# Layer 0's second activation: integer codes transposed by DMA in place of TensorE transposes

## The chip, the cores and the metric
One Trainium2 chip, one core. The metric is the device time of one execution in microseconds (us); three runs of the kernel before gave 379.6, 379.04 and 378.78, median 379.04. An execution under the profiler took 380.96 us.

## The reference
Input: x of 8 sequences x 512 tokens x 256 features. Two layers, each x = x + ffn(cond(x)). In layer 0, cond is an adapter chosen by a language id (256 to 64, ReLU, back to 256, residual) and a layer norm. The feed-forward part is two "bitlinear" maps with GELU between them:

```python
w_scale = clip(mean(abs(W)), EPS, None)
Wq = clip(round(W / w_scale), -1, 1) * w_scale           # ternary weights
x_scale = clip(max(abs(x), axis=-1), EPS, None)          # one per token
xq = clip(round(x * (127 / x_scale)), -128, 127) * (x_scale / 127)
y = einsum('bnd,hd->bnh', xq, Wq) + b                    # 256 -> 1024, GELU, 1024 -> 256
```

Layer 1 has a linear map chosen by a subject id, and a feed-forward part of the same kind with a depthwise convolution of three taps and SiLU in the middle.

## The kernel before, in words
Tokens lie on the 128 partitions. A block is 128 tokens; a pair is two blocks (k = 0 and 1); a batch (one sequence) is two pairs; there are 16 pairs. Every engine has its own program, written out by hand and executed in order; semaphores tie them. Layer 0 is a software pipeline of slots: slot (i, sp) works on pair 2i+sp in stage 0 (adapter, layer norm), on the pair before in stage 1 (rounding and transposing z), on the one before that in stage 2 (`up1`, `gelu`, `absmax1`, `scale1`, `inverse1`, `round1`) and on the one three back in stage 3 (`transpose1`, `untranspose`, `down1`, `final1`). I call (i,0) an even slot and (i,1) an odd one. At the end of an odd slot `adapter_in` (TensorE, L1133) computes the adapter's first map for the next batch; `adapter_out` (L1145) its second, once a slot; VectorE adds the result to the tokens (L809).

Stage 2 ends with `round1` on GpSimd (POOL): it multiplies GELU's output by the token's scale and adds the constant `ROUND`, 3*2^22 + 0x6600, in fp32, so that the low 16 bits of each word are the fp16 number 1536 + q, q the rounded integer. In stage 3 TensorE transposes those halves, 8 times 128x128 fp16 into one PSUM bank (`transpose1`, L1191); ScalarE (ACT) takes 1536 off again and writes q as bf16 to `q1T` (`untranspose`, L511); `down1` (L1200) multiplies by the ternary weights `w_dn0` in 8 matmuls that add up in PSUM; VectorE scales, adds the residual and writes `x1` (`final1`, L958), and SP stores x1 (L345).

SP issues all loads of layer 0. Its slots are: in an even slot `load_adapter_in(i+1)` (xT, cw1, cb1 of the next batch), in an odd one `load_tokens(i+1)` (cw2 at L323, cb2 at L324, the tokens xtok at L328, gamma and beta at L331 and L332); then in both the store of the pair in stage 3. Each of these buffers exists once, so a load waits until the present batch is through with it. A load that depends on a language id is preceded by a `value_load` of the id into a register. In layer 0, SP has no other work; i runs from 0 to 6 for the loads. Behind the last loads come `load2(0)` and the last stores.

POOL's order in a slot is `split_scales`, `residual` (L664), `scale_of_up`, `round1` of block 0, `inverse_deviation`, `round1` of block 1. VectorE's order is in `slot` at L898 to L928. Between the layers, `seam` writes out by hand how the last pairs of layer 0 mix with the first batch of layer 1.

Of the kernel before, what the change touches and what calls it, by code (L numbers as in the profile page):

```python
# [10 lines left out]
F16 = mybir.dt.float16  # L11
BF16 = mybir.dt.bfloat16
I32 = mybir.dt.int32

P = 128

# [1 line left out]
OFFSET = 1536.0  # L18
ROUND = float(3 << 22) + 0x6600
QMAX = 127.0  # L20
QEPS = 1e-5
LN_EPS = 1e-5


def build_program(nc, t):
# [12 lines left out]
    with ExitStack() as ctx:  # L38
        def sb(name, shape, dt=F32):
            return ctx.enter_context(nc.sbuf_tensor(name, shape, dt))  # L40

        def sem(name):
            return ctx.enter_context(nc.semaphore(name))
# [21 lines left out]
        idb = sb("idb", [P, P], BF16)  # L65
        ones = sb("ones", [P, P])
        nhalf = sb("nhalf", [P, 2])
        ids_sb = sb("ids_sb", [1, 2 * B], I32)
        raw_all = sb("raw_all", [P, 4, KD * H])
        raw = [raw_all[:, n, :] for n in range(4)]  # L70
# [49 lines left out]
        qs1 = [sb(f"qs1_{k}", [P, 1]) for k in range(2)]  # L120
        dq1 = [[sb(f"dq1_{r}_{k}", [P, 1]) for k in range(2)] for r in range(2)]
        r1 = [sb(f"r1_{k}", [P, H]) for k in range(2)]
        q1T = [sb(f"q1T{k}", [P, KH, P], BF16) for k in range(2)]
        xb = sb("xb", [P, PAIRS, 2, D])

# [4 lines left out]
        BANK_W = [7, 1, 7, 1]  # L130

        s_const = sem("s_const")
        s_ident = sem("s_ident")
        s_ones = sem("s_ones")
        s_hone = sem("s_hone")
# [37 lines left out]
        s_s1 = sems("s_s1", 2)  # L173
        s_qs1 = sems("s_qs1", 2)
        s_r1 = sems("s_r1", 2)
        s_t1 = sems("s_t1", 2)
        s_q1T = sems("s_q1T", 2)
        s_dn = sems("s_dn", 2)
        s_x1 = sems("s_x1", 2)
# [122 lines left out]
        def _(sp):  # L302
# [16 lines left out]
            def load_tokens(b, s):  # L319
# [11 lines left out]
                sp.dma_start(gam[:, :], t["gamma"][bass.ds(lang, 1), :].to_broadcast([P, D])).then_inc(s_ldgb, 16)  # L331
                sp.dma_start(bet[:, :], t["beta"][bass.ds(lang, 1), :].to_broadcast([P, D])).then_inc(s_ldgb, 16)  # L332

            def slot(i, sp_):

                if not isinstance(i, int) or 0 <= i < B - 1:
                    if sp_ == 0:
                        load_adapter_in(i + 1)
                    else:
                        load_tokens(i + 1, 2 * i + 2)  # L340
                if (c := in_slot(i, sp_, 3, PAIRS)):

                    n, par, h = c
                    sp.wait_ge(s_x1[1], n + 1)
                    sp.dma_start(item(scratch, h)[:, 2 * par:2 * par + 2, :], x1[par][:, :, :]) \  # L345
                        .then_inc(s_st1[par], 16)

            def load2(b):
# [56 lines left out]
        def _(act):  # L405
# [27 lines left out]
            def slot(i, sp):  # L433
                a1, a2, b_, c_ = (in_slot(i, sp, lag, PAIRS) for lag in range(4))

                def round_z():

                    n, par, h = a2
                    act.wait_ge(s_qsz, n + 1)
                    wait(act, s_zT, n)  # L440
                    for k in range(2):
                        ins = act.activation(rz[:, k, :], z[par][:, k, :], ACT.Copy, scale=qsz[par][:, k:k + 1],
                                             bias=ROUND)
                    ins.then_inc(s_rz, 1)
# [12 lines left out]


                second = isinstance(i, int) and (i, sp) == (1, 0)
                coming = a1 if second else in_slot(i, sp, -1, PAIRS) if sp == 1 else None  # L460
                if isinstance(i, int) and (i, sp) == (0, 1):
                    coming = None
                if second:
                    if b_:
                        gelu(b_, 0)
                    if coming:
                        adapter_hidden(coming)
                    if a2:
                        round_z()
                        untranspose_z()  # L470
                    if b_:
                        gelu(b_, 1)
                    return
                if b_:
                    gelu(b_, 0)
                if c_:
                    untranspose(c_, 0)
                if a2:
                    round_z()
                if b_:  # L480
                    gelu(b_, 1)
                if c_:
                    untranspose(c_, 1)
                if a2:
                    untranspose_z()
                if coming:
                    adapter_hidden(coming)
# [9 lines left out]
            def gelu(b_, k):  # L497
# [4 lines left out]
                wait(act, s_r1[k], n)  # L502
                act.activation(g1[k][:, :], bank(BANK_UP + 2 * k, 2), ACT.Gelu,  # L503
                               scale=dqz[par][:, k:k + 1]).then_inc(s_gelu[k], 1)

            def untranspose(c_, k):

                n, par, h = c_
                act.wait_ge(s_t1[k], n + 1)
                wait(act, s_dn[k], n)  # L510
                act.activation(q1T[k][:, :, :].rearrange("p k c -> p (k c)"),  # L511
                               bank16(BANK_T1, F16)[:, :], ACT.Copy, bias=-OFFSET).then_inc(s_q1T[k], 1)

            def lead(b, k):
                act.wait_ge(p_xT[k], b + 1)
# [40 lines left out]
            def seam():  # L556
                slot(B, 0)
                gelu(pair(PAIRS - 1), 0)
                lead(0, 0)
                untranspose(pair(PAIRS - 2), 0)  # L560
                gelu(pair(PAIRS - 1), 1)
                lead(0, 1)
                untranspose(pair(PAIRS - 2), 1)
                untranspose(pair(PAIRS - 1), 0)
                untranspose(pair(PAIRS - 1), 1)

            def slot2(s):
                on(lead_scales, s - 1)
# [33 lines left out]
        def _(pool):  # L602
# [7 lines left out]

            pool.memset(ones[:, :], 1.0).then_inc(s_ones, 1)
            pool.memset(nhalf[:, :], -0.5).then_inc(s_ident, 1)

            pool.memset(bias9b[:, :], 0.0).then_inc(s_b9z, 1)
            for k in range(2):
# [4 lines left out]
            def slot(i, sp):  # L620
# [56 lines left out]
                if b_:  # L677
                    round1(b_, 1)

            def round1(b_, k):  # L680

                n, par, h = b_
                wait(pool, s_t1[k], n)
                pwait(s_qs1[k], n + 1)
                pool.tensor_scalar(r1[k][:, :], g1[k][:, :], qs1[k][:, 0:1], ROUND, ALU.mult, ALU.add) \  # L685
                    .then_inc(s_r1[k], 1)

                pwait(s_x1[k], n - 1)
                pool.tensor_scalar(dq1[par][k][:, :], s1[k][:, :], ws[:, 1:2], 0.0, ALU.mult, ALU.add) \
                    .then_inc(s_dq1[k], 1)  # L690

            def round_y(b, k):
# [60 lines left out]
                on(tap_sum, s, 0)  # L753
                on(middle_tap, s, 2)

            run(slot, seam, slot2, pool)

        @block.vector
        def _(dve):
# [351 lines left out]
        def _(pe):  # L1111
# [66 lines left out]
                    ins = pe.matmul(o, c[:, k, :], bias9b[:, m * 512:(m + 1) * 512], start=False, stop=True)  # L1178
                ins.then_inc(s_up[k], 1)

            def transpose1(c_, k):
                n, par, h = c_
                if isinstance(n, int) and (n, k) == (0, 0):

                    pe.wait_ge(s_tern[1], 1)
                    pe.wait_ge(s_wsc, 7)
                pe.wait_ge(s_r1[k], n + 1)
                wait(pe, s_q1T[1 - k], n if k == 0 else n + 1)
                r16 = r1[k][:, :].bitcast(F16)
                for c in range(KH):  # L1190
                    ins = pe.transpose(bank16(BANK_T1, F16)[:, c * P:(c + 1) * P],  # L1191
                                       r16[:, 2 * c * P:2 * (c + 1) * P:2], id16[:, :])
                ins.then_inc(s_t1[k], 1)

            def down1(c_, k):
                n, par, h = c_
                pe.wait_ge(s_q1T[k], n + 1)
                wait(pe, s_x1[1 - k], n if k == 0 else n + 1)
                for c in range(KH):
                    ins = pe.matmul(bank(BANK_DN)[:, k * D:(k + 1) * D], q1T[k][:, c, :], w_dn0[:, c, :],  # L1200
                                    start=(c == 0), stop=(c == KH - 1))
                ins.then_inc(s_dn[k], 1)

            def slot(i, sp):
# [16 lines left out]
                    return  # L1221
                if b_:
                    up1(b_, 0)
                if c_:
                    transpose1(c_, 0)
                if a1:
                    adapter_out(a1)
                if b_:
                    up1(b_, 1)
                if c_:  # L1230
                    transpose1(c_, 1)
                if a2:
                    transpose_z(a2)
                if c_:
# [108 lines left out]
            def seam():  # L1343
                slot(B, 0)
                up1(pair(PAIRS - 1), 0)
                transpose_x(0, 0)
                transpose1(pair(PAIRS - 2), 0)
                up1(pair(PAIRS - 1), 1)
                linear(0, 0)
                transpose_x(0, 1)  # L1350
                transpose1(pair(PAIRS - 2), 1)
                down1(pair(PAIRS - 2), 0)
                linear(0, 1)
                down1(pair(PAIRS - 2), 1)
                transpose1(pair(PAIRS - 1), 0)
                spread_scales(0)
                transpose1(pair(PAIRS - 1), 1)
                transpose_y(0)
                down1(pair(PAIRS - 1), 0)
                down1(pair(PAIRS - 1), 1)  # L1360
# [87 lines left out]
```

## Time and profile before

| | |
|---|---|
| median of 3 runs | 379.04 us (378.78 to 379.6) |
| profiled execution | 380.96 us, its span 379.2 us |
| mean granted TensorE clock | 0.923 |
| layer 0, one batch (two slots) | 16.73 us |
| busy: TensorE / VectorE / ScalarE / GpSimd | 79% / 81% / 65% / 72% |

The span runs from the first instruction to the last. Times in the views below are microseconds from its start unless marked ns. PE is TensorE, PEld its weight loads, DVE VectorE, ACT ScalarE, POOL GpSimd, SPq the queue of SyncE that issues DMAs. Ends of pipelined matmuls are modelled, so busy times of PE overlap a little; the chain of waits gives the net time of a pass.

### The profile page before, as it was taken

How to read it: one execution, taken by the hardware profiler on the slowest of the kernel's cores; microseconds unless marked ns; L12 is line 12 of the kernel's file. 1: busy time of each engine (PE TensorE's matmuls, PEld its weight loads, DVE VectorE, ACT ScalarE, POOL GpSimd, SP SyncE). 2: the span in 40 equal slices, each digit the busy share in tenths (PEclk: the TensorE clock that was granted, in tenths of full speed). 3: DMA queues.
4: the chain of work that ended last, by engine and by line, in shares of the span. 5: the costliest groups of instructions: out<-in, count | busy, mean ns of one | idle time of the engine just before them, and what ended most of it. 6: DMA issues, size and time to landing. Idle time of an engine off the chain costs nothing.

```text
span 379.2 us, 7190 instructions
## 1 busy us (share of the span) xinstructions
PE 298.0 (79%) x2104; PEld 206.4 (54%) x2104; DVE 306.6 (81%) x649; ACT 246.1 (65%) x325; POOL 272.0 (72%) x433
## 2 busy tenths in 40 slices
PE   0449598999999898894482969898898979778694
PEld 0125356556565565472251647676776767556573
DVE  0875979899999999755169889999899999989563
ACT  3354657666676767553122678797979888788583
POOL 1342576777677777535055999999999999999921
PEclk9858989999999999996676889999999999989799
DMA  8980232424243330400542110014050502121201
GB/s 223 262 275 14 72 122 87 162 71 152 92 119 125 116 118 28 126 28 29 179 170 82 55 43 0 31 62 147 16 185 26 181 30 71 42 71 42 86 28 69
DMA packets 29421, 36.36 MB, mean 96 GB/s; under 512 B 6582, under 2 KB 22718, under 8 KB 29383
## 3 DMA queue, kind: packets, MB, share of 16 engines
q1 hardware_dynamic: 25142, 31.50, 25.6%
q10 hardware_dynamic: 4240, 4.41, 4.2%
q8 instruction: 17, 0.28, 0.3%
q14 instruction: 22, 0.17, 0.2%
HBM read 27.51 MB, written 8.39 MB: 95 GB/s over the span
## 4 chain that ended last, share of the span: by engine, by line
PE 35%; POOL 29%; issue 20%; DVE 6%; DMA 5%; ACT 3%; ACTq 1%; POOLq 0%; DVEq 0%; SPq 0%
POOL mid L712 12%; POOL raw_all L719 8%; PE banks L1200 8%; PE banks L1177 6%; POOL xb L696 5%; PE banks L1133 4%; PE banks L1178 3%; PE banks L1191 3%; PE banks L1145 3%; DMA raw_all<-in_w2b 3%; PE banks L1269 2%; DMA convb<-in_convb 2%; PE banks L1339 1%; DVE x L958 1%; PE banks L1157 1%
## 5 line engine op out<-in xcount | busy, mean ns | idle before, releaser
L719 POOL TENSOR_TENSOR raw_all<-raw_all,mid 128x1024 f32<-128x1024 f32 x32 | 77.0, 2407 | 3.7 <-DVE raw_all L1003 2.1
L685 POOL TENSOR_SCALAR r<-g,qs 128x1024 f32<-128x1024 f32 x32 | 36.0, 1124 | 41.9 <-DVE qs L949 41.7
L536 ACT ACTIVATE banks<-xb,taps 128x512 f32<-128x512 f32 x64 | 42.9, 687 | 30.6 <-DVE xb L996 30.5
L712 POOL TENSOR_SCALAR mid<-xb,taps,convb 128x512 f32<-128x512 f32 x64 | 49.3, 778 | 14.5 <-DVE xb L996 14.4
L503 ACT ACTIVATE g<-banks,dqz 128x1024 f32<-128x1024 f32 x32 | 35.5, 1109 | 31.2 <-PE banks L1178 29.8
L996 DVE TENSOR_TENSOR xb<-banks,dqb 128x512 f32<-128x512 f32 x64 | 42.5, 685 | 12.0 <-PE banks L1302 11.8
L1003 DVE SCALAR_TENSOR_TENSOR raw_all<-xb,taps,banks 128x512 f32<-128x512 f32 x64 | 46.9, 742 | 0.7 <-ACT banks L536 0.5
L934 DVE TENSOR_REDUCE am<-g 128x1 f32<-128x1024 f32 x32 | 38.7, 1208 | 5.9 <-ACT g L503 5.8
L1302 PE MATMUL banks<-yT,tern 128*128 128x512 bf16 x128 | 38.7, 410 | 2.8 <-DVE raw_all L1003 1.7
L1200 PE MATMUL banks<-tern,q1T 128*128 128x256 bf16 x256 | 35.3, 283 | 6.0 <-DVE x L958 6.0
L1009 DVE TENSOR_REDUCE am<-g 128x1 f32<-128x1024 f32 x32 | 38.6, 1206 | 1.6 <-ACT g L542 1.6
L1177 PE MATMUL banks<-tern,qT 128*128 128x512 bf16 x128 | 38.1, 379 | 0.9 <-ACT qcT L455 0.9
L542 ACT ACTIVATE g<-banks 128x1024 f32<-128x1024 f32 x32 | 32.6, 1018 | 8.6 <-POOL r L725 4.2
L1313 PE MATMUL banks<-id,raw_all 128*128 128x128 f32 x256 | 35.5, 284 | 0.6 <-ACT g L542 0.5
L1339 PE MATMUL banks<-tern,q1T 128*128 128x256 bf16 x256 | 35.0, 282 | 0.8 <-DVE o L1030 0.7
L511 ACT ACTIVATE q1T<-banks 128x1024 bf16<-128x1024 f16 x32 | 32.6, 1017 | 4.5 <-PE banks L1191 4.5
L1313 PEld LDWEIGHTS banks<-id,raw_all 128*128 128x128 f32 x256 | 31.0, 147 | 5.7 <-ACT g L542 1.5
L553 ACT ACTIVATE q1T<-banks 128x1024 bf16<-128x1024 f16 x32 | 32.6, 1020 | 1.5 <-PE banks L1325 1.5
L1200 PEld LDWEIGHTS banks<-tern,q1T 128*128 128x128 bf16 x256 | 23.5, 101 | 18.0 <-ACT q1T L511 7.4
L1269 PE MATMUL banks<-wl,x2T 128*128 128x256 f32 x128 | 32.7, 400 | 0.8 <-issue 0.7
L1325 PE MATMUL banks<-id,r 128*128 128x128 f16 x256 | 20.5, 225 | 11.6 <-POOL r L725 9.9
L1269 PEld LDWEIGHTS banks<-wl,x2T 128*128 128x128 f32 x128 | 24.7, 199 | 7.9 <-ACT x2T L517 2.4
(102 smaller groups left out, 630.8 us busy)
## 6 DMA issues: line engine op xcount, KB each, us to landing
xT<-in_xT SPq DMA_DIRECT2D x8, 512.0 KB, 3.7
xtok<-in_x SPq DMA_DIRECT2D x8, 512.0 KB, 3.6
x_after_layer<-x SPq DMA_DIRECT2D x16, 256.0 KB, 2.1
x<-x_after_layer SPq DMA_DIRECT2D x8, 512.0 KB, 4.3
xr<-x_after_layer SPq DMA_DIRECT2D x8, 512.0 KB, 3.7
out_y<-o SPq DMA_DIRECT2D x32, 128.0 KB, 1.7
wl<-in_cwl SPq DMA_DIRECT2D x8, 256.0 KB, 3.8
raw_all<-in_w1a ACTq DMA_DIRECT2D x1, 1024.0 KB, 5.1
```

The source lines that it names most:

```text
L536: act.activation(bank(BANK_U + f % 2), apad[:, f, 2:S + 2], ACT.Copy, scale=taps[:, f, 2:3]).then_inc(p_last, 1)
L712: pool.tensor_scalar(mid[f // 2 % 2][:, f % 2, :], apad[:, f, 1:S + 1], taps[:, f, 1:2], convb[:, f:f + 1], ALU.mult, ALU.add).then_inc(p_ ...
L719: pool.tensor_tensor(c[:, 2 * q:2 * q + 2, :], c[:, 2 * q:2 * q + 2, :], mid[q % 2][:, :, :], ALU.add).then_inc(p_sum, 1)
L934: dve.tensor_reduce(am1[k][:, :], g1[k][:, :], AX_X, ALU.max, apply_absolute_value=True) \
L996: dve.tensor_tensor(apad[:, f, 1:S + 1], bank(BANK_U + f % 2), dqb[b % 2][:, :], ALU.mult) \
L1003: dve.scalar_tensor_tensor(out=conv[b % 2][:, f, :], in0=apad[:, f, 0:S], scalar=taps[:, f, 0:1], in1=bank(BANK_U + f % 2), op0=ALU.mult, ...
L1177: pe.matmul(o, q[:, k, j, :], w_up0[:, j, m * 512:(m + 1) * 512], start=(j == 0), stop=False)
L1200: ins = pe.matmul(bank(BANK_DN)[:, k * D:(k + 1) * D], q1T[k][:, c, :], w_dn0[:, c, :], start=(c == 0), stop=(c == KH - 1))
L1269: ins = pe.matmul(bank(BANK_Y)[:, a * D:(a + 1) * D], x2T[:, 2 * k + a, j, :], wl1[par][:, j, :], start=(j == 0), stop=(j == KD - 1))
L1302: ins = pe.matmul(bank(BANK_U + f % 2), w_up1[:, k, f * P:(f + 1) * P], yT[b % 2][:, k, :], start=(k == 0), stop=(k == KD - 1))
L1313: ins = pe.transpose(bank(BANK_C + f // KT)[:, (f % KT) * P:(f % KT + 1) * P], conv[b % 2][:, f, k * P:(k + 1) * P], id32[:, :])
L1339: ins = pe.matmul(bank(BANK_D2)[:, (k % 2) * D:(k % 2 + 1) * D], q2T[k % 2][:, f, :], w_dn1[:, f, :], start=(f == 0), stop=(f == KH - 1))
```

## The change
For the second activation of layer 0 only (pair by pair, both blocks):

- `round1` on POOL writes q + 128 as a 16-bit unsigned integer (`r1u`, the first half of the old buffer). It now waits for the block's previous DMA transpose in place of the TensorE transpose.
- SP gets `transpose1`: for each block one DMA transpose of 128 x 1024 16-bit elements from `r1u[k]` to `q1T[k]`. TensorE's `transpose1` and ScalarE's `untranspose` are gone, also from the seam.
- SP's slot is reordered: in an even slot `load_adapter_in`, the transposes of blocks 0 and 1, the store; in an odd slot the transpose of block 0, `load_tokens`, the transpose of block 1, the store.
- `down1` reads the transposed integers as fp16 bits: the integer n is then n * 2^-24. A ninth matmul with the constant -128 * 2^-24 (`uncode`) and the column sums of the ternary weights (`colsum0`) takes the 128 off. The factor 2^24 goes into `dq1`.
- POOL computes `colsum0` once, with three additions after slot (1,0).

```diff
+        colsum0 = sb("colsum0", [P, 4, D], BF16)
+        r1u = [r1[k][:, 0:H // 2].bitcast(U16) for k in range(2)]
...
+            def transpose1(b_, k):
+                n, par, h = b_
+                sp.wait_ge(s_r1[k], n + 1)
+                wait(sp, s_dn[k], n)
+                sp.dma_start_transpose(q1T[k][:, :, :].bitcast(U16), r1u[k][:, :]).then_inc(s_q1T[k], 16)
+
             def slot(i, sp_):
...
+                b_, c_ = (in_slot(i, sp_, lag, PAIRS) for lag in (2, 3))
+                if 0 <= i < B - 1 and sp_ == 0:
+                    load_adapter_in(i + 1)
+                if b_:
+                    transpose1(b_, 0)
+                if 0 <= i < B - 1 and sp_ == 1:
+                    load_tokens(i + 1, 2 * i + 2)
+                if b_:
+                    transpose1(b_, 1)
+                if c_:
+                    n, par, h = c_
                     sp.wait_ge(s_x1[1], n + 1)
...
-            def untranspose(c_, k):
...
+            pool.memset(uncode[:, :], -CODE * UNIT).then_inc(s_uncode, 1)
...
+            def column_sums0():
+
+                pool.wait_ge(s_tern[1], 1)
+                for n, (a, c, o) in enumerate(((w_dn0[:, 0:4, :], w_dn0[:, 4:8, :], colsum0[:, :, :]),
+                                               (colsum0[:, 0:2, :], colsum0[:, 2:4, :], colsum0[:, 0:2, :]),
+                                               (colsum0[:, 0, :], colsum0[:, 1, :], colsum0[:, 0, :]))):
+                    wait(pool, s_colsum, n)
+                    pool.tensor_tensor(o, a, c, ALU.add).then_inc(s_colsum, 1)
...
-                wait(pool, s_t1[k], n)
+                wait(pool, s_q1T[k], 16 * n)
                 pwait(s_qs1[k], n + 1)
-                pool.tensor_scalar(r1[k][:, :], g1[k][:, :], qs1[k][:, 0:1], ROUND, ALU.mult, ALU.add) \
+                pool.tensor_scalar(r1u[k][:, :], g1[k][:, :], qs1[k][:, 0:1], CODE, ALU.mult, ALU.add) \
...
-            def transpose1(c_, k):
...
+                pe.wait_ge(s_q1T[k], 16 * (n + 1))
+                wait(pe, s_x1[1 - k], n if k == 0 else n + 1)
+                o = bank(BANK_DN)[:, k * D:(k + 1) * D]
                 for c in range(KH):
-                    ins = pe.matmul(bank(BANK_DN)[:, k * D:(k + 1) * D], q1T[k][:, c, :], w_dn0[:, c, :],
-                                    start=(c == 0), stop=(c == KH - 1))
+                    pe.matmul(o, q1T[k][:, c, :].bitcast(F16), w_dn0[:, c, :], start=(c == 0), stop=False)
+                ins = pe.matmul(o, uncode[:, :], colsum0[:, 0, :], start=False, stop=True)
                 ins.then_inc(s_dn[k], 1)
```

## Rows read from the trace of the kernel before

**Rows 1.** The page, engines: busy us (share), instructions.
```profile
PE 298.0 (79%) x2104; PEld 206.4 (54%) x2104; DVE 306.6 (81%) x649; ACT 246.1 (65%) x325; POOL 272.0 (72%) x433
```
**Rows 2.** Chain of waits in order of time: start, us, what.
```profile
83.61 1.86 PE banks L1133 x4
...
87.74 0.45 PE banks L1191 x8
88.19 0.92 PE banks L1145 x4
...
91.28 0.99 PE banks L1200 x8
...
92.93 1.03 PE banks L1200 x8
...
99.36 0.98 PE banks L1200 x8
...
195.35 1.83 PE banks L1269 x8
```
**Rows 3.** Table by stretches: stretch, us, busy us of each engine, clock, DMA.
```profile
82.90:91.28 8.38, 8.38 (x58) 4.82 (x56) 7.67 (x21) 5.41 (x9) 6.48 (x17) 1.00 0.44 136
91.28:99.64 8.36, 7.29 (x59) 4.86 (x59) 7.80 (x21) 6.29 (x10) 5.91 (x15) 1.00 0.29 101
```
**Rows 4.** SP's queue in order of time: start, us.
```profile
5.97 0.47 SPq L323 DMA_DIRECT2D cw_sb<-in_cw  x1
...
6.99 0.38 SPq L328 DMA_DIRECT2D xtok<-in_x  x1
...
96.76 0.34 SPq L345 DMA_DIRECT2D x_after_layer<-x  x1
97.86 0.47 SPq L323 DMA_DIRECT2D cw_sb<-in_cw  x1
98.52 0.33 SPq L324 DMA_DIRECT2D cw_sb<-in_cb  x1
99.97 0.38 SPq L328 DMA_DIRECT2D xtok<-in_x  x1
```
**Rows 5.** VectorE in order of time: start, us, instruction.
```profile
56.60 0.68 DVE L809 TENSOR_TENSOR xx<-xtok,banks 128x512 f32<-128x512 f32 x1
...
90.07 0.68 DVE L809 TENSOR_TENSOR xx<-xtok,banks 128x512 f32<-128x512 f32 x1
...
99.69 0.15 DVE L949 RECIPROCAL qs<-s 128x1 f32<-128x1 f32 x1
...
106.80 0.68 DVE L809 TENSOR_TENSOR xx<-xtok,banks 128x512 f32<-128x512 f32 x1
```
**Rows 6.** POOL in order of time.
```profile
45.12 0.27 POOL L689 TENSOR_SCALAR dq<-s,ws 128x1 f32<-128x1 f32 x1
45.57 0.19 POOL L629 CAST qshi<-qsz 128x2 bf16<-128x2 f32 x1 [0.18 <-DVE qsz L867]
...
48.27 1.13 POOL L685 TENSOR_SCALAR r<-g,qs 128x1024 f32<-128x1024 f32 x1
...
100.11 1.13 POOL L685 TENSOR_SCALAR r<-g,qs 128x1024 f32<-128x1024 f32 x1
```
**Rows 7.** From issue to landing: xtok (L328), the store (L345), taps (L423).
```profile
DMA to landing us min/median/max: 3.4/3.6/4.3
...
DMA to landing us min/median/max: 2.0/2.1/3.9
...
DMA to landing us min/median/max: 6.6/6.6/6.6
```
**Rows 8.** Groups of instructions: busy us, mean ns, idle before.
```profile
L511 ACT ACTIVATE q1T<-banks 128x1024 bf16<-128x1024 f16 x32 | 32.6, 1017 | 4.5 <-PE banks L1191 4.5
L719 POOL TENSOR_TENSOR raw_all<-raw_all,mid 128x1024 f32<-128x1024 f32 x32 | 77.0, 2407 | 3.7 <-DVE raw_all L1003 2.1
L685 POOL TENSOR_SCALAR r<-g,qs 128x1024 f32<-128x1024 f32 x32 | 36.0, 1124 | 41.9 <-DVE qs L949 41.7
L632 POOL COPY qc<-qshi 128x6 bf16<-128x6 bf16 x16 | 3.1, 195 | 0.0
L629 POOL CAST qshi<-qsz 128x2 bf16<-128x2 f32 x16 | 3.0, 186 | 7.1 <-DVE qsz L867 4.7 <-PE banks L1160 2.4
L614 POOL MEMSET bias9b<- 128x1024 bf16 x1 | 1.0, 952 | 0.0
```
**Rows 9.** Seam, in order of time.
```profile
177.55 1.91 PE L1200 MATMUL banks<-tern,q1T 128*128 128x256 bf16 x8
```

More of the change, by code:

```diff
@@ L13 @@
 I32 = mybir.dt.int32
+U16 = mybir.dt.uint16
 P = 128
@@ L20 @@
 QMAX = 127.0
+CODE = 128.0
+UNIT = 2.0 ** -24
 QEPS = 1e-5
@@ L67, in build_program @@
         nhalf = sb("nhalf", [P, 2])
+        uncode = sb("uncode", [P, P], BF16)
         ids_sb = sb("ids_sb", [1, 2 * B], I32)
@@ L132, in build_program @@
         s_const = sem("s_const")
+        s_colsum = sem("s_colsum")
+        s_uncode = sem("s_uncode")
         s_ident = sem("s_ident")
@@ L175, in build_program @@
         s_r1 = sems("s_r1", 2)
-        s_t1 = sems("s_t1", 2)
         s_q1T = sems("s_q1T", 2)
@@ L332, in load_tokens @@
                 sp.dma_start(bet[:, :], t["beta"][bass.ds(lang, 1), :].to_broadcast([P, D])).then_inc(s_ldgb, 16)
-            def slot(i, sp_):
[L336 to L343, printed above, removed]
+            def transpose1(b_, k):
[3 more added lines that the diff above has]
+                sp.dma_start_transpose(q1T[k][:, :, :].bitcast(U16), r1u[k][:, :]).then_inc(s_q1T[k], 16)
+            def slot(i, sp_):
+                b_, c_ = (in_slot(i, sp_, lag, PAIRS) for lag in (2, 3))
[9 more added lines that the diff above has]
+                    n, par, h = c_
                     sp.wait_ge(s_x1[1], n + 1)
-                    sp.dma_start(item(scratch, h)[:, 2 * par:2 * par + 2, :], x1[par][:, :, :]) \
+                    sp.dma_start(scratch[h][:, 2 * par:2 * par + 2, :], x1[par][:, :, :]) \
                         .then_inc(s_st1[par], 16)
@@ L475, in slot @@
                     gelu(b_, 0)
-                if c_:
-                    untranspose(c_, 0)
                 if a2:
@@ L481, in slot @@
                     gelu(b_, 1)
-                if c_:
-                    untranspose(c_, 1)
                 if a2:
@@ L504, in gelu @@
                                scale=dqz[par][:, k:k + 1]).then_inc(s_gelu[k], 1)
-            def untranspose(c_, k):
[L508 to L512, printed above, removed]
             def lead(b, k):
@@ L559, in seam @@
                 lead(0, 0)
-                untranspose(pair(PAIRS - 2), 0)
                 gelu(pair(PAIRS - 1), 1)
                 lead(0, 1)
-                untranspose(pair(PAIRS - 2), 1)
-                untranspose(pair(PAIRS - 1), 0)
-                untranspose(pair(PAIRS - 1), 1)
             def slot2(s):
@@ L678, in slot @@
                     round1(b_, 1)
+            def column_sums0():
[5 more added lines that the diff above has]
+                    pool.tensor_tensor(o, a, c, ALU.add).then_inc(s_colsum, 1)
             def round1(b_, k):
                 n, par, h = b_
-                wait(pool, s_t1[k], n)
+                wait(pool, s_q1T[k], 16 * n)
                 pwait(s_qs1[k], n + 1)
-                pool.tensor_scalar(r1[k][:, :], g1[k][:, :], qs1[k][:, 0:1], ROUND, ALU.mult, ALU.add) \
+                pool.tensor_scalar(r1u[k][:, :], g1[k][:, :], qs1[k][:, 0:1], CODE, ALU.mult, ALU.add) \
                     .then_inc(s_r1[k], 1)
                 pwait(s_x1[k], n - 1)
-                pool.tensor_scalar(dq1[par][k][:, :], s1[k][:, :], ws[:, 1:2], 0.0, ALU.mult, ALU.add) \
+                pool.tensor_scalar(dq1[par][k][:, :], s1[k][:, :], ws[:, 1:2], 1.0 / UNIT, ALU.mult, ALU.mult) \
                     .then_inc(s_dq1[k], 1)
@@ L754, in slot2 @@
                 on(middle_tap, s, 2)
-            run(slot, seam, slot2, pool)
+            run(slot, seam, slot2, pool, after={2: column_sums0})
         @block.vector
@@ L1179, in up1, with down1 @@
                 ins.then_inc(s_up[k], 1)
-            def transpose1(c_, k):
+            def down1(c_, k):
                 n, par, h = c_
@@ L1186, in transpose1 @@
                     pe.wait_ge(s_wsc, 7)
-                pe.wait_ge(s_r1[k], n + 1)
-                wait(pe, s_q1T[1 - k], n if k == 0 else n + 1)
-                r16 = r1[k][:, :].bitcast(F16)
-                for c in range(KH):
[L1191 to L1199, printed above, removed]
-                    ins = pe.matmul(bank(BANK_DN)[:, k * D:(k + 1) * D], q1T[k][:, c, :], w_dn0[:, c, :],
-                                    start=(c == 0), stop=(c == KH - 1))
+                    pe.wait_ge(s_uncode, 1)
+                    pe.wait_ge(s_colsum, 3)
+                pe.wait_ge(s_q1T[k], 16 * (n + 1))
+                wait(pe, s_x1[1 - k], n if k == 0 else n + 1)
+                o = bank(BANK_DN)[:, k * D:(k + 1) * D]
+                for c in range(KH):
+                    pe.matmul(o, q1T[k][:, c, :].bitcast(F16), w_dn0[:, c, :], start=(c == 0), stop=False)
+                ins = pe.matmul(o, uncode[:, :], colsum0[:, 0, :], start=False, stop=True)
                 ins.then_inc(s_dn[k], 1)
@@ L1223, in slot @@
                     up1(b_, 0)
-                if c_:
-                    transpose1(c_, 0)
                 if a1:
@@ L1229, in slot @@
                     up1(b_, 1)
-                if c_:
-                    transpose1(c_, 1)
                 if a2:
@@ L1346, in seam @@
                 transpose_x(0, 0)
-                transpose1(pair(PAIRS - 2), 0)
                 up1(pair(PAIRS - 1), 1)
@@ L1350, in seam @@
                 transpose_x(0, 1)
-                transpose1(pair(PAIRS - 2), 1)
                 down1(pair(PAIRS - 2), 0)
@@ L1354, in seam @@
                 down1(pair(PAIRS - 2), 1)
-                transpose1(pair(PAIRS - 1), 0)
                 spread_scales(0)
-                transpose1(pair(PAIRS - 1), 1)
                 transpose_y(0)
```

## The prediction, made before the change was timed
> **What bounds the kernel now.** The page comes first: VectorE is the busiest engine (81%), TensorE next (79%), and nothing is full [rows 1]. These are averages over two layers, and the change touches layer 0 only, so I read its steady part, where work repeats every two slots (one batch, two pairs of row blocks). In the chain of waits that stretch is TensorE nearly throughout: each pass of 8 down matmuls takes 0.98 us, each pass of 8 transposes 0.45, the adapter's second matmuls 0.92, its first ones 1.86 once per batch [rows 2]. The table by stretches gives two slots as 8.38 + 8.36 us, with TensorE busy 8.38 and 7.29 and VectorE 7.67 and 7.80 [rows 3]. So TensorE ends last, and VectorE is some 0.6 us a slot behind it: that is the most a relief of TensorE alone can give. The same is seen from VectorE's queue: the addition of the adapter's result to the tokens (L809) recurs at 90.07 and 106.80, a period of 16.73 us [rows 5].
>
> Then SP's queue, which the change rearranges. Today it is early: for the next batch the adapter's second weights (cw2) are issued at 97.86, cb2 at 98.52, the tokens (xtok) at 99.97 [rows 4], and they are needed at about 104.9 (adapter_out, one period after 88.19 [rows 2]) and 106.80 [rows 5].
>
> **What goes.** TensorE loses two passes of 0.45 us a slot, ScalarE two of 1017 ns [rows 2, 8]. ScalarE has idle time (5.41 and 6.29 busy of 8.4 [rows 3]), so its 2 us a slot are worth nothing. TensorE gains a ninth matmul for each block, 0.98/8 = 0.12 us: net 2 x (0.45 - 0.12) = 0.66 a slot. That would be a gain of up to 1.2 to 1.3 us a batch if nothing new came last.
>
> **What is added in each block.** A DMA transpose of 256 KB on SP's queue. POOL's rounding writes 16-bit integers instead of fp32: 1124 ns now; the small cast and copy on POOL do not differ (186 and 195 ns) [rows 8], a memset of 1024 bf16 takes 952, so 0.95 to 1.12, and I take no change. fp16 bits as stationary operand: the present transposes load fp16 at TensorE's ordinary pace, 0.45 us for 8 of 128 columns against 0.98 for 8 of 256, so I take no change; the other end is the fp32 pass of L1269, 8 matmuls in 1.83 us against 0.98 [rows 2], which would cost 0.85 a block and be hidden in the loop below.
>
> **The loop that I expect to end last.** SP's program is in order. In the odd slot (i,1) it now reads: wait for the rounding of block 0, transpose it, then value_load, cw2, cb2, xtok, gamma, beta, then the transpose of block 1, then the store. Behind the new wait stand the loads of the next batch, each with a single buffer, for which TensorE and VectorE wait. Rounding of block 0 in that slot begins at 100.11 and takes 1.13: it ends at 101.24 [rows 6]. From there, per batch:
> - wake-up 0.1 (an estimate), and D, the time by which a transpose holds back what is queued behind it;
> - value_load 0.76 (store issued 96.76 + 0.34, cw2 at 97.86), then 1.02 from cw2 to xtok where no wait intervenes (L323 at 5.97, L328 at 6.99) [rows 4];
> - xtok lands 3.6 us after its issue [rows 7], and L809 starts: sum 5.48 + D;
> - from L809 of the even slot (90.07) through a densely filled VectorE queue to the reciprocal at 99.69 [rows 5] and the end of the rounding at 101.24: 11.17.
>
> The loop is 16.65 + D, against 16.73 now. The branch through cw2 is as long: cb2 lands some 0.65 + 2.1 after cw2's issue (landing estimated by the shortest row, the store's), adapter_out 1.08, VectorE's start 0.2: 4.0 in place of 4.6. So TensorE's relief vanishes in any case, and every batch pays about D.
>
> D is not in this trace. Lower end: the issue of an ordinary DMA of the same 256 KB, 0.33 us, if the rings swallow it [rows 4]. Upper end: the slowest landing of a DMA cut in about a thousand pieces (taps, 12 KB), 6.6 us [rows 7]; a transpose of 128 rows by 8 groups of 128 columns has at least 1024. Nearest is the store of 256 KB on this very queue, 2.1 us from issue to landing [rows 7]: following loads ride the same rings. I take D = 2.1: +2.0 us a batch. Loads follow transposes for i = 1 to 6; the first falls in the start-up, five remain: +10.1.
>
> [...]
>
> **Start-up.** POOL adds the column sums after slot (1,0), that is after 45.12 + 0.27 = 45.4: additions over 1024, 512 and 256 elements. Upper, at the pace of the fp32 two-input row L719, 2407 ns for 1024: 1792 elements in 4.2, with two waits 4.4; lower, at the single-input pace of L685, 2.0 [rows 6, 8]. I take 4.4, the same kind of instruction. Behind it stand split_scales (45.57 now) and with it transpose_z, dqz, and the rounding of pair 1: 48.27 + 1.13 + 4.25 = 53.65 [rows 6]. Add 5.48 + D = 7.58: VectorE's addition for pair 4 starts at 61.2, now 56.60 [rows 5]: +4.6 (D's first share is in it).
>
> **Other moves.** The transpose of block 1 in the odd slot is ready to go at 105.1, but SP reaches it after beta: 101.34 + 2.1 + 0.76 + 1.02 to xtok, 1.3 more for the issues of xtok, gamma and beta = 106.5, landing 108.6 or, behind the 512 KB of xtok, near 110. Its matmuls were at 109.67 (92.93 and one period [rows 2]) and move back by 2: just covered. Block 0's has over 6 us (101.24 to 108.0, that is 91.28 and one period [rows 2, 6]) and is covered up to D near 4. The store moves behind a transpose; its buffer is free for two slots. After the last loads (slots (7,0) to (8,0)) TensorE's relief does show: about -1.0. At the seam the last down passes run at half clock (1.91 us for 8 [rows 9]) and wait for POOL's round_y anyway; the ninth matmuls cost 2 x 0.24: +0.5.
>
> **Sum:** 4.6 + 10.1 - 1.0 + 0.5 = +14.2 us. The profiled execution took 380.96 us (span 379.2): 395.2, and since it lies 1.9 above the median of the runs, 379.04, I state 393.2. With D = 0.33: 2.8 + 1.25 - 0.5 = +3.6, 382.6. With D = 4.5: 7.0 + 22.1 - 0.5, 407.6.
>
> **Rivals.**
> 1. The relief comes through: loads land in time after all, and VectorE's 7.67 + 7.80 = 15.5 sets the period. About -1.0 x 7 batches, + 2.5 for POOL's start-up: 374.5. It is decided at SP: the loop must fall below 15.5, that is D plus xtok's landing under 2.5 us, where the fastest landing of xtok alone is 3.4. For it: SP is idle most of the time today. It needs the rounding of block 0 to come clearly earlier, which VectorE's order forbids. Chance 0.12, with 0.03 more for an exact balance.
> 2. The transposes fill the queue. Four a batch: from 4D > 16.65 + D, that is D above 5.6, they set the period. With 6.6: 26.4 a batch, +9.7 x 6.5 = 63, and 9 at the start: 451. For it: taps' 6.6 us for 12 KB; against it: it was issued right behind the 1 MB of w1a and 128 KB of b2a. Chance 0.09. [...]
> 3. POOL's sums are hidden or quick while the loop holds: 2.4 less, 391.
> The forecast with its D of 0.33 to 5.6, rival 3 included, has 0.76.
>
> **Numbers.** 393, range 382 to 411: D from 0.3 to 5. Less than 0.2% (0.8 us) cannot be told from no change. Slower 0.85, same 0.03, faster 0.12.
>
> **What would show it.** Right: in the odd slot the issue of cw2 stands right behind the first transpose; TensorE idles before adapter_out of even slots or VectorE before the addition, released by a DMA; period near 18.7; POOL has 4.4 us of additions near 45. Wrong: period under 16.7 in layer 0, or idle time before the down matmuls released by the transposes (then latency or the queue, not the order on SP, sets the time).

## The result, and the profile after

The changed kernel takes 398.52 us (median of 4 runs, 394.44 to 401.18) against 378.91 for the kernel before (4 runs, 378.54 to 379.6): ratio 1.042, interval 1.0379 to 1.0461, so it is slower. Every ratio here leaves out runs more than 1.5% above the fastest of their kernel (two of the four of the changed kernel, and five of the twelve of e7_spread, whose profiled run is one of them), while the medians in the table below are of all runs. The two others, 394.44 and 396.25, stand against a forecast of 393.2, and the profiled one, 396.25, against 395.2. Its span is 394.2 us, 15.0 more than before.

First the page, engines, in answer to [rows 1]: TensorE and ScalarE have less to do, as intended, and every share has fallen.
```profile
PE 290.3 (74%) x1880; PEld 195.5 (50%) x1880; DVE 307.6 (78%) x649; ACT 218.7 (55%) x293; POOL 276.4 (70%) x437
```
SP's queue in one odd slot (start, us), in answer to [rows 4]. The transpose of block 0 waits until 91.46; cw2, cb2 and xtok are issued only behind it.
```profile
88.50 0.57 SPq L361 DMA_DIRECT2D x_after_layer<-x  x1
91.46 1.25 SPq L346 DMA_TRANSPOSE q1T<-r  x1
94.02 0.50 SPq L331 DMA_DIRECT2D cw_sb<-in_cw  x1
94.70 0.34 SPq L332 DMA_DIRECT2D cw_sb<-in_cb  x1
95.14 0.41 SPq L336 DMA_DIRECT2D xtok<-in_x  x1
```
The chain of waits through the same stretch (start, us, what) is the loop of the prediction, link by link: rounding, transpose, value_load (L316), cw2 and cb2, the landing of xtok, VectorE's addition.
```profile
90.31 1.13 POOL r L695
91.46 1.25 SPq L346
...
92.75 0.80 SPq L316
...
94.02 0.50 SPq L331
...
94.70 0.34 SPq L332
...
95.14 3.46 DMA xtok<-in_x
...
98.69 0.06 DVE xx L819
```
VectorE's addition, in answer to [rows 5]: its start moves from 80.48 to 98.69, a period of 18.21 us in place of 16.73, and it idles for the load.
```profile
80.48 0.69 DVE L819 TENSOR_TENSOR xx<-xtok,banks 128x512 f32<-128x512 f32 x1 [1.71 <-DMA xtok<-in_x]
98.69 0.69 DVE L819 TENSOR_TENSOR xx<-xtok,banks 128x512 f32<-128x512 f32 x1 [1.40 <-DMA xtok<-in_x]
```
That period as a row of the table by stretches, in answer to [rows 3] (us; busy of PE, PEld, DVE, ACT, POOL; clock; DMA): no engine is busy for more than 15.6 of 18.2 us.
```profile
80.48:98.69 18.21, 14.19 (x84) 8.09 (x82) 15.55 (x40) 8.05 (x14) 12.62 (x31) 1.00 0.69 163
```
POOL at the start, in answer to [rows 6]: the sums take 4.0 us, and split_scales begins at 49.05 in place of 45.57.
```profile
45.00 2.12 POOL L688 TENSOR_TENSOR colsum<-tern 128x1024 bf16<-128x1024 bf16 x1
47.20 1.90 POOL L688 TENSOR_TENSOR colsum<-colsum 128x512 bf16<-128x512 bf16 x2
49.05 0.18 POOL L630 CAST qshi<-qsz 128x2 bf16<-128x2 f32 x1
```
The new instruction, from the view of its line (ns min/median/max), and its time from issue to landing:
```profile
L346 SPq DMA_TRANSPOSE q1T<-r x32: 1232/1250/2644, 41.0 to 186.9; - x32
...
DMA to landing us min/median/max: 3.1/3.3/4.7
```

To compare kernels I cut each profiled execution in three by the same events: the start (VectorE's first addition L809 to that of pair 4), five batches (to that of pair 14), and the seam (from that of pair 15 to the first transposes of layer 1's second batch, 186.32 in the kernel before). Times in us; "median" and "before" are of one session on one chip.

| kernel | start | five batches | seam | median | before |
|---|---|---|---|---|---|
| before | 40.72 | 83.67 | 37.81 | | 378.91 |
| changed | 46.15 | 93.62 | 39.31 | 398.52 | 378.91 |
| e1_order | 45.37 | 83.85 | 37.56 | 384.20 | 378.35 |
| e2_nosums | 42.06 | 93.87 | 37.59 | 394.46 | 378.35 |
| e3_half | 45.87 | 91.24 | 37.61 | 393.09 | 378.35 |
| e4_notrans | 45.26 | 82.34 | 37.60 | 385.28 | 378.35 |
| e6_order_swap | 44.74 | 82.94 | 36.82 | 383.79 | 377.71 |
| e7_spread | 40.94 | 85.52 | 37.76 | 380.37 | 377.71 |
| e8_before_swap | 37.19 | 80.98 | 36.46 | 372.79 | 377.71 |
| e9_double | 47.20 | 105.72 | 37.97 | 409.59 | 377.71 |
| e10_notrans_swap | 44.19 | 79.55 | 36.46 | 381.08 | 380.52 |
| e11_all_nosums | 38.42 | 86.12 | 37.75 | 379.37 | 380.52 |
| e12_swap_again | 39.14 | 81.02 | 36.82 | 375.46 | 380.52 |

So the 15.0 us are +5.4 at the start, +9.95 in five batches, -0.2 from pair 14 to pair 15 (the one slot between the stretches of the table, 8.24 to 8.04), +1.5 in the seam, and -1.7 in layer 1. The last two are no effect of the change. The seam's 1.5 us are of that one execution: no later kernel with DMA transposes shows them. Layer 1 from its second batch on, which no kernel here changes, takes between 189.6 and 193.0 us in the thirteen profiled executions. The start scatters too: e8_before_swap and e12_swap_again are the same kernel and differ by 1.95 us there, all of it ahead of the addition of pair 3. Where the start matters I therefore also give the time from the addition of pair 3 to that of pair 4: 10.13 us in the kernel before, 15.89 in the changed one.

### The profile page after: what moved, and what is told of

It is laid out like the page before. It is cut to its first block, busy times and chain, and to the rows that moved or that the text cites. A ratio compares the mean times of both kernels' runs of the same rounds, so it can differ in the third digit from the quotient of the medians.

```text
span 394.2 us, 6716 instructions
## 1 busy us (share of the span) xinstructions
PE 290.3 (74%) x1880; PEld 195.5 (50%) x1880; DVE 307.6 (78%) x649; ACT 218.7 (55%) x293; POOL 276.4 (70%) x437
## 3 DMA queue, kind: packets, MB, share of 16 engines
q1 hardware_dynamic: 58934, 39.89, 38.3%
## 4 chain that ended last, share of the span: by engine, by line
POOL 34%; issue 25%; PE 15%; DMA 10%; DVE 8%; SPq 4%; ACT 3%; ACTq 1%; POOLq 0%; DVEq 0%
POOL mid L722 11%; POOL raw_all L729 8%; DMA xtok<-in_x 5%; POOL xb L706 4%; POOL r L695 3%; PE banks L1202 3%; DMA raw_all<-in_w2b 2%; PE banks L1267 2%; DMA convb<-in_convb 2%; SPq L346 2%; POOL xb L665 2%; PE banks L1187 1%; PE banks L1143 1%; SPq L316 1%; POOL rstd L659 1%
## 5 line engine op out<-in xcount | busy, mean ns | idle before, releaser
L695 POOL TENSOR_SCALAR r<-g,qs 128x1024 uint16<-128x1024 f32 x32 | 35.8, 1119 | 41.7 <-DVE qs L959 41.6
L1006 DVE TENSOR_TENSOR xb<-banks,dqb 128x512 f32<-128x512 f32 x64 | 42.5, 685 | 10.9 <-PE banks L1300 10.1
L1187 PE MATMUL banks<-tern,qT 128*128 128x512 bf16 x128 | 39.4, 390 | 0.9 <-ACT qcT L471 0.9
L665 POOL TENSOR_TENSOR xb<-xtok,b2f 128x512 f32<-128x512 f32 x16 | 21.1, 1321 | 20.9 <-DMA xtok<-in_x 20.9
L1202 PEld LDWEIGHTS banks<-tern,q1T 128*128 128x128 f16 x256 | 24.0, 103 | 21.3 <-DMA q1T<-r 8.1
L557 ACT ACTIVATE q1T<-banks 128x1024 bf16<-128x1024 f16 x32 | 32.6, 1020 | 1.5 <-PE banks L1323 1.5
L968 DVE SCALAR_TENSOR_TENSOR x<-banks,dq,xb 128x256 f32<-128x256 f32 x32 | 15.4, 480 | 17.3 <-PE banks L1203 17.3
```

What stands on the lines that cost most here:

```text
L695: pool.tensor_scalar(r1u[k][:, :], g1[k][:, :], qs1[k][:, 0:1], CODE, ALU.mult, ALU.add) \
L1006: dve.tensor_tensor(apad[:, f, 1:S + 1], bank(BANK_U + f % 2), dqb[b % 2][:, :], ALU.mult) \
L1187: pe.matmul(o, q[:, k, j, :], w_up0[:, j, m * 512:(m + 1) * 512], start=(j == 0), stop=False)
L1202: pe.matmul(o, q1T[k][:, c, :].bitcast(F16), w_dn0[:, c, :], start=(c == 0), stop=False)
```

## The experiments

**e1_order: loads ahead of the transpose.** Only SP's order changes.
```diff
+                if loads:
+                    lang = load_tokens(i + 1, 2 * i + 2)      # cw2, cb2, xtok
                 if b_:
                     transpose1(b_, 0)
-                if 0 <= i < B - 1 and sp_ == 1:
-                    load_tokens(i + 1, 2 * i + 2)
+                if loads:
+                    load_norm(i + 1, 2 * i + 2, lang)         # gamma, beta
```


> The changed kernel with one reordering on SP: in the odd slot cw2, cb2 and xtok are issued before the wait and the transpose of block 0, gamma and beta stay behind it. Theory A (the transpose, its wait and the value_load hold back the loads of the next batch): xtok's landing disappears from the chain, the batch period falls from 18.2 to 19.5 us to about 16.5, and with five to six batches some 11 to 14 us go: 396.25 becomes 382 to 386 in the profile. Rival B (the transposes' own landing, 3.3 us, or the rings set the time): block 0's matmuls still wait for its transpose and the time stays above 392.

Measured: 384.20 us, 1.0148 of before (1.0089 to 1.0206). As theory A has it: five batches fall from 93.62 to 83.85 us, within 0.2 of the kernel before. The order on SP is the cause of the steady part's loss: shown. But the period is 16.77, not the 16.5 I hoped for: TensorE's relief brings nothing.

**e9_double: the suspected cost twice.** The transpose of block 0 is issued twice, first into a spare buffer; POOL's next rounding of the block waits for both.
```diff
                 wait(sp, s_dn[k], n)
+                if k == 0:
+                    wait(sp, s_spare, 16 * n)
+                    sp.dma_start_transpose(spare[:, :, :].bitcast(U16), r1u[k][:, :]).then_inc(s_spare, 16)
```


> The changed kernel with the transpose of block 0 issued twice (the first into a spare buffer), so that the time by which it holds back SP is doubled. Theory A: each of the five periods with loads grows by one issue, 1.25 to 1.5 us, and the start by one: +7 to +9, 403 to 405. Rival B (rings or landing set the time): the growth is at least the full landing, 3.3 us a batch, +16 or more, or none if the loop is elsewhere.

Measured: 409.59 us, 1.085 of before (1.0818 to 1.0882), 13 to 15 above the changed kernel's 394.44 and 396.25, and 12.6 in the profiled executions (408.84 against 396.25): more than the 7 to 9 of theory A and less than the 16 of rival B. The chain decides between them. Over one batch:
```profile
95.72 1.12 POOL r L702
...
96.86 1.25 SPq L350
...
98.16 1.31 SPq L351
...
99.51 0.79 SPq L318
...
101.88 3.38 DMA xtok<-in_x
...
105.36 0.06 DVE xx L826
```
Both issues stand in the chain one behind the other, and landing does not: SP's time is what counts, as theory A has it. The period from 84.82 to 105.36 is 20.54, 2.3 above 18.21: 1.3 is the second issue, about 1.1 more lies between the addition (84.82) and the rounding's end (96.85), 12.03 against 10.96. The trace shows where that comes from. Because cw2 is later still, TensorE stands idle for 2.67 us before adapter_out, against 1.38 in the changed kernel, and behind it the granted clock (the last column but two of the table by stretches) is 0.50 (of 850 stretches of 0.2 us of the changed kernel, from 30 to 200, 741 show 1.00 and 100 show 0.50):
```profile
84.15:85.43 1.28, 1.28 (x4) 0.45 (x3) 0.61 (x2) 0.00 (x0) 0.64 (x1) 0.50 0.89 211
86.31 1.47 PE L1209 MATMUL banks<-tern,q1T 128*128 128x256 bf16 x8
```
That pass takes 1.05 us in the changed kernel. With the ninth matmul behind it, block 0's product is ready at 87.88, and VectorE's `final1` starts at 87.92; the scale that it reads was computed a slot earlier. So the doubled issue costs more than its own time: behind the longer wait TensorE's pass also took 1.47 us in place of 1.05.

**e3_half: half the columns.**
```diff
-                sp.dma_start_transpose(q1T[k][:, :, :].bitcast(U16), r1u[k][:, :])
+                sp.dma_start_transpose(q1T[k][:, 0:KH // 2, :].bitcast(U16), r1u[k][:, 0:H // 2])
```


> Each DMA transpose moves 512 columns instead of 1024 (the other half of q1T is a constant, so half of the product is left out). If the issue time on SP grows with the columns, it falls from 1.25 to about 0.65 us, and each batch gains that once in the loop and perhaps once more where SP is late: -4 to -7 us, near 390. If it is a fixed cost, SP still takes 1.25 us and the time stays within 1 us of 396.

```profile
L346 SPq DMA_TRANSPOSE q1T<-r x32: 1189/1204/1493, 43.5 to 184.4; - x32
...
DMA to landing us min/median/max: 2.4/2.5/5.8
```
The issue takes 1204 ns in place of 1250: between these two widths nearly a fixed cost of some 1.2 us on SP, where one that grows with the columns would have halved. The landing falls from 3.3 to 2.5 us. Five batches are 2.4 us shorter and the median is 393.09 (391.88 to 397.54), a gain between those of the two cases; part of it is a shorter value_load in this trace (0.50 in place of 0.80), which I can't account for.

**e2_nosums: no column sums.**
```diff
+            pool.memset(colsum0[:, 0, :], 0.0).then_inc(s_colsum, 3)
-            run(slot, seam, slot2, pool, after={2: column_sums0})
+            run(slot, seam, slot2, pool)
```


> The changed kernel without POOL's three additions: colsum0 is set to zero by a memset in the preamble, so the correction by 128 times the column sums is left out. Theory A: POOL's 4.03 us stand on the path at the start (split_scales begins at 49.05 in place of 45.57), so 3 to 3.5 us go: about 392.5 to 393. Rival: the start is held by the second transpose of block 0 waiting for the first down matmuls, so under 1 us goes.

The start falls by 4.09 us (from pair 3 to pair 4 alone by 4.64, from 15.89 to 11.25); the five batches stay (93.87). The whole time does not show it: the four runs, 392.02 to 396.12, lie about where the changed kernel's 394.44 and 396.25 do, and the ratio to the kernel before is 1.0404 against 1.042. It is the trace of the start that shows POOL's sums on the path: TensorE's transpose_z waits for split_scales behind them. The rival named a true wait as well, since in both traces the transpose of block 0 waits for the first down matmuls; but these wait for transpose_z, and so for the sums.

**e4_notrans: what the removal is worth if nothing replaces it.**
```diff
                 if b_:
-                    transpose1(b_, 0)
+                    pass
...
-                pe.wait_ge(s_q1T[k], 16 * (n + 1))
+                pe.wait_ge(s_r1[k], n + 1)
```


> No transposes at all: TensorE waits for the rounding and reads a constant q1T, so the product is left out of the result; the POOL sums, the ninth matmul and SP's order of loads stay. This is what the removal of the TensorE transposes and ScalarE copies is worth where nothing replaces them. Theory A: period 15.5 to 16.2 us (VectorE's 15.55 busy plus small waits), about -5 against the kernel before in layer 0, +3.5 at the start: 375 to 379. Rival (TensorE's relief is worth nothing because VectorE's order sets the period already): period 16.7, about 382.

Measured: 385.28 us, above the kernel before (1.0175, 1.0113 to 1.0238), and above both expectations. The start carries the sums. The five batches take 82.34, a period of 16.47, nearer to the rival's 16.7 than to theory A: the removal of TensorE's transposes and ScalarE's copies is worth 0.27 us a batch, not 1.2. TensorE in the odd slot shows where the rest went (in brackets: idle time before, and its releaser):
```profile
102.15 0.38 PE L1189 MATMUL banks<-bias9b,qcT 128*128 128x512 bf16 x1
103.70 0.38 PE L1168 MATMUL banks<-id,rz 128*128 128x128 f16 x4 [1.17 <-ACT rz L458]
...
104.22 1.05 PE L1203 MATMUL banks<-tern,q1T 128*128 128x256 bf16 x8
```
It reaches transpose_z early and waits for ScalarE's rounding of z, which waits for VectorE; down1 stands behind it in the program though it could run.

**e6_order_swap: fill that wait.** e1 with one exchange on TensorE.
```diff
-                if a2:
-                    transpose_z(a2)
                 if c_:
                     down1(c_, 0)
+                if a2:
+                    transpose_z(a2)
```


> e1_order with one more change on TensorE: in every slot down1 of block 0 stands before transpose_z. Theory A2 (the time freed on TensorE is lost in its wait for ScalarE's round_z, 1.2 to 1.5 us in the odd slot, because nothing independent stands ahead of transpose_z): the wait is filled, the batch period falls from 16.77 to 15.7 to 16.0 us and about 5 us go: 377 to 379. Rival (VectorE's order alone sets the period): it stays at 16.7 and the time at 384.

Measured: 383.79 us, 1.0156 of before (1.0116 to 1.0197), no better than e1. That is the rival's number, but not for its reason: in six of ten slots the period is now about 8.03 us (half of 16.06). In three of the others (9.63, 8.43 and 8.40 us) down1 now comes early enough to wait for its DMA transpose, by up to 3.68 us; the fourth, 8.38 us, e8 has too. The longest wait:
```profile
82.75 1.05 PE L1207 MATMUL banks<-tern,q1T 128*128 128x256 bf16 x8 [3.68 <-DMA q1T<-r]
```
That slot takes 9.63 us. The table of stretches for this kernel shows the DMA engines' share and GB/s (last two columns) while it waits: with a transpose, the load of beta and a store under way, they move almost nothing for about two us, and the transpose lands 6.1 us after its issue in place of 3.3.
```profile
78.00:79.00 1.00, 1.00 (x12) 0.72 (x10) 1.00 (x4) 0.80 (x1) 1.00 (x3) 1.00 3.13 191
79.00:80.00 1.00, 0.07 (x2) 0.00 (x0) 0.96 (x6) 0.85 (x2) 1.00 (x3) 1.00 0.12 1
80.00:81.00 1.00, 0.00 (x0) 0.00 (x0) 1.00 (x2) 0.00 (x0) 1.00 (x2) 1.00 1.67 34
81.00:82.00 1.00, 0.00 (x0) 0.00 (x0) 0.45 (x2) 0.00 (x0) 0.83 (x3) 1.00 0.39 80
```

**e8_before_swap: the same exchange in the kernel before.** The diff is e6's, applied to the old TensorE slot, with its transposes in place.

> The kernel before with the same exchange on TensorE (down1 of block 0 before transpose_z). Theory A2: there TensorE is busy with its transposes while round_z runs, the wait before transpose_z is only 0.4 us, so the period stays at 16.7 and the time within 1 us of 379 (transpose_z later by 1 us may even cost a little). Rival (the exchange is a gain of its own): 3 us or more go.

This expectation failed, and taught most: the rival held. It takes 372.79 us against 377.71, ratio 0.9885 (0.9852 to 0.9919): faster than both kernels. TensorE's odd slot:
```profile
93.92 0.61 PE L1191 MATMUL banks<-id,r 128*128 128x128 f16 x8
94.37 1.04 PE L1200 MATMUL banks<-tern,q1T 128*128 128x256 bf16 x8
95.25 0.39 PE L1157 MATMUL banks<-id,rz 128*128 128x128 f16 x4
```
transpose_z starts 0.88 us behind down1's start and needs no wait. The 0.4 us of waiting before it were not all the exchange could save. The chain of waits no longer runs through TensorE but round POOL and VectorE:
```profile
93.80 0.19 POOL qshi L629
...
95.06 1.22 POOL xb L664
...
96.49 1.13 POOL r L685
...
98.22 0.68 POOL rstd L658
...
99.57 0.48 DVE z L843
...
101.08 0.36 DVE sz L860
...
101.54 0.18 DVE qsz L867
...
101.84 0.19 POOL qshi L629
```
From one `split_scales` to the next it is 101.84 - 93.80 = 8.04 us a slot; the additions lie 8.03 apart, 16.06 a batch. This loop contains neither TensorE nor ScalarE.

**e12_swap_again: the same, timed again.**

> e8_before_swap unchanged, timed again beside the two others and with more rounds: 372 to 374, 1.0 to 1.5% under the kernel before.

375.46 us against 380.52 in that session, ratio 0.9886 (0.9834 to 0.9938). The ratio repeats; both kernels are 2.7 to 2.8 us slower than in the session before, so 375.46 lies above the 372 to 374 expected.

**e10_notrans_swap: the removal once more, beside e8's order.** e4 with the exchange.

> e4_notrans (no transposes at all, TensorE reads a constant q1T, so the product is left out) with down1 of block 0 before transpose_z. Theory A3: with that exchange the loop POOL - VectorE - POOL of 8.03 us a slot sets the period, with TensorE's transposes in place as without them, so their removal is worth nothing: period 16.06 as in e8_before_swap, and a time of e8's 372.8 plus the 4 us of POOL's sums plus 1 for the constant's memset, 377 to 379. Rival (TensorE is still part of the bound in e8): period 15.6 or less and under 375.

Five batches take 79.55 us, a mean period of 15.91 against 16.20 in e8 and e12. Half of that difference are two slots of 8.36 and 8.38 us which e10 doesn't have; the plain slots take 7.96 in place of 8.03, 0.14 us a batch. The chain of waits in e10 is the same loop of POOL and VectorE, its links a little shorter, without TensorE. So with that loop ahead, TensorE's transposes cost 0.14 to 0.3 us a batch: near theory A's nothing, far from the 15.6 of the rival. The time, 381.08 us, is 2 to 4 above the expected one (the session's 2.8 us are part of that) and 5.6 above e12. The sums make that up: from pair 3 to pair 4 it takes 13.57 us against 7.96.

**e7_spread: the sums in POOL's gaps.** e6 with seven additions of 256 columns, two ahead of the first round1, two and three behind inverse_deviation; pair 0 uses the weights themselves.
```diff
+                if at == (1, 0):
+                    sums0(0, 2)
                 if b_:
                     round1(b_, 0)
...
+                if n == 0:
+                    for c in range(KH):
+                        ins = pe.matmul(o, uncode[:, :], w_dn0[:, c, :], start=False, stop=(c == KH - 1))
```


> e6_order_swap with the column sums cut into 7 additions of 256 columns in POOL's gaps of slots (1,0) and (1,1); pair 0 multiplies the constant with all 8 weight tiles instead. Theory A: 2.5 to 3.5 us of the start go: 374 to 376, faster than both kernels. Rival (the start is held elsewhere, by q1T's buffer or a cold TensorE): under 1 us goes.

The start falls by 3.8 us to 40.94, that of the kernel before. The ratio is 1.0029 (1.0001 to 1.0056), the median of all twelve runs 380.37, above the 374 to 376 expected: every cost that was found is mended and it is still no gain. The profiled execution, 382.53 us, is one of the longer ones (376.58 to 385.14). In it one slot takes 11.66 us: the DMA engines stand nearly still as above, TensorE waits 3.64 us for its transpose, and its granted clock is 0.50 from 79 to 85. How often that happens in the shorter executions no trace shows.

**e11_all_nosums: the three costs away together.** e6 with e2's edit.

> e6_order_swap without POOL's sums (colsum0 zero, so the correction by the column sums is left out): all three costs of the change that were found taken away together. Theory: it stands at e6's 383.8 minus 3.5 to 4, 379.5 to 380.5, still above e8_before_swap by 6 to 7, because the transposes land 3.3 us after their issue and the queue stands still now and then. Rival (DMA transposes cost nothing once their place is right): within 1 us of e8, 372 to 374.

379.37 us, ratio 0.9997 (0.9957 to 1.0038): equal to the kernel before, and 3.9 above e12, less than the 6 to 7 expected and more than the rival's 1. In the profiled execution (382.11, one of the longest of ten) most slots take 8.03 us; two take 11.26 and 10.15, 5.3 us lost. In both TensorE waits for a late transpose (3.71 and 2.80 us), and its granted clock is 0.50 for most of three to four us afterwards.

## Why the prediction was right

The direction, the place and the mechanism were right: the loop through SP's queue sets the period in the steady part (e1), with SP's issue in it and not the landing (e9). That the total fits so well is partly luck. By the prediction's own steps:

- **The loop through SP** [rows 4 to 7]: predicted 16.65 + D with D = 2.1, 18.75; measured 18.21 in the shortest batch. The single terms were off both ways. The wake-up behind the rounding is 0.02 us (91.44 to 91.46), not 0.1; D is 1.25 us of SP's time, not 2.1; value_load with its gaps takes 1.31 (92.71 to 94.02), not 0.76; xtok lands in 3.5.
- **Five batches**: +9.95 against +10.1, and here the luck lies. Five times 18.21 would be +7.4. The other 2.6 us come from things that the prediction did not have: the five periods are 18.46, 18.21, 19.46, 19.01 and 18.48. In the third a transpose holds SP for 2.64 us (at 109.68). TensorE then stands idle for 2.25 us before adapter_out, its granted clock falls (0.56 on average from 115.4 to 119.3), and so the fourth is long too. In the first and the last xtok lands 0.3 us later. A D that was too large made up for them.
- **The start**: predicted +4.6 with D in it, measured +5.4, or +5.8 from pair 3 to pair 4. The sums are worth 4.09 to 4.64 (e2), where I had 4.25 behind split_scales. The addition of pair 4 comes at 62.02, not 61.2. From the transpose on, value_load with its gaps takes 1.70 (not 0.76) and xtok lands in 4.40 (not 3.6), against a D of 1.25 (not 2.1). There was also a wait that I had overlooked: in slot (1,1) the rounding of block 0 ends at 52.85, but its transpose waits for `s_dn[0]`, since q1T has one buffer per block and the first down matmuls end only at 53.34. They take 1.82 us, at a granted clock of 0.50, TensorE having stood idle for 7.97 us before transpose_z (in the kernel before the same pass takes 1.75):
```profile
51.29 1.82 PE banks L1202 x8
...
53.42 1.24 SPq L346
```
- **After the last loads**: predicted -1.0 for TensorE's relief over three slots and +0.5 at the seam. Of that only one slot can be read by itself, -0.2 from pair 14 to pair 15. With the seam the changed kernel is 1.3 longer there, but e1, with the same TensorE program, 0.5 shorter, so the sum of -0.5 is not refuted.
- **What the relief is worth.** "TensorE ends last" [rows 2, 3] was true of the chain but not of what its relief is worth. I took VectorE's busy time (15.5 a batch) as the next bound; the runs put 16.06 there, a loop of POOL and VectorE with all its wake-ups (e8), and before it a wait of 1.17 us for round_z, in which the transposes had stood at almost no cost (e4). Rival 1 with its 374.5 was therefore out of reach even with loads in time: e1 had them in time and took 384.2. The forecast did not rest on this, since the loop through SP hid the relief.
- **Other moves**: the transposes' landings were covered in the changed kernel to the extent predicted (TensorE's weight loads waited 5.6 us in all for them between 60 and 150, four times, ahead of block 1's matmuls). The changed kernel's SP queue carries 58934 packets against 25142, so 1056 for each of the 32 transposes, where the prediction had at least 1024; rival 2 (the queue is full) still did not occur.

Left open: why transposes sometimes land late. In e6, e7 and e11 the DMA engines nearly stop for one and a half to two us with a transpose under way, four times in all (79.0 to 80.5 in e6). Each time an instruction fetch (a packet of the queue q8, which the view marks "instruction") starts within 0.3 us of it; but two more fetches in e6 (at 100.3 and 126.9), also with a transpose under way, pass without a stop, so the fetch alone is not shown to be the cause. In the changed kernel such a stop is not shown: its engines move nothing from 108.6 to 110.4, where the transpose of 2.64 us is issued, but neither do they in the undisturbed batch (0 GB/s from 90.5 to 92.5). Why that issue takes longer is open as well.

## What to carry to other kernels

Here a wait put into SP's in-order queue, ahead of the loads, made a batch 18.21 us instead of the 16.77 with the loads ahead of it (e1): trace the loop from such a wait round to itself, since its length is the new period. Time taken off the engine on the chain is worth only what the next loop allows, and here that loop, 16.06 us a batch (e8), was longer than the busy time of VectorE, the busiest engine, about 15.5; look first for an instruction that waits while an independent one stands behind it. Here two steps exchanged on TensorE gave 1.1%, and the whole DMA route gave nothing. And when a forecast comes out right, compare it term by term: here two errors met.

## What the runs showed of the hardware

- A DMA transpose of 128 x 1024 16-bit elements from SBUF to SBUF held SP for 1.25 us (median of 32, changed kernel), where the plain DMAs of the kernel before took 0.33 to 0.48 (80 to 110 of its trace); with 512 columns it was 1.20 (e3). It landed 3.3 us after its issue, with 512 columns 2.5 (medians of 32). Some issues of the changed kernel took longer: 1.5 us behind the loads of gamma and beta (1.53 at 96.66), once 2.64 (at 109.68).
- Plain stores issued right behind transposes took SP 0.56 to 0.78 us, mostly 0.57 (changed kernel), in place of 0.33, and value_load plus the gaps around it 1.31 (92.71 to 94.02) in place of 0.76 (97.10 to 97.86 in the kernel before).
- Integers up to 255, stored in 16 bits and read by TensorE as fp16 (all of them below the smallest normal fp16 number), were multiplied at the same pace as the bf16 integers before: 0.98 us for 8 matmuls of 256 columns in both kernels (at 110.73 in the changed one, at 99.36 in the one before).
- A wait of TensorE cost more than its length in three traces. After idle times of 2.25, 2.67 and 3.71 us (the changed kernel, e9, e11) its granted clock went to 0.50: adapter_out took 1.62 us in the changed kernel in place of 1.10, and a pass of 8 matmuls took 1.47 us in e9 and 1.88 in e11 in place of 1.05; after one of 3.68 us in e6 it stayed at 1.00.
- POOL added two bf16 inputs a little faster than two fp32 ones: 2.12 us for 1024 columns (L688 of the changed kernel at 45.00), against 2407 ns (L719 of the kernel before) [rows 8].
